# Narrow causal attention on one Trainium2 core: probabilities turned undivided, value products multiplied by inverted sums that a DMA spreads over the partitions

## The reference, cut to what matters

```
x = x + 0.5 * _L0_ffn(layernorm(x))      # narrow causal attention, then 16 experts, top 4
x = x + _L0_attn(layernorm(x))           # heads of 8
x = x + 0.5 * _L0_ffn(layernorm(x))      # the same narrow attention and experts again
x = x + 0.5 * _L1_ffn(layernorm(x))
x = x + _L1_attn(layernorm(x))           # wide attention: heads of 128, two blocks of keys
x = x + 0.5 * _L1_ffn(layernorm(x))
```

```
q, k = rope((h @ wq), (h @ wk)); v = h @ wv      # 32 query heads, 8 key heads of 64
scores = q k^T / 8, causal over 512 positions
attn = softmax(scores)
x = x + (attn @ v) @ wo
```

## Time and profile before

| | us |
|---|---|
| median of 3 runs | 3932.72 (3931.78 to 3938.23) |
| the profiled execution | 3977.27 |
| its span, first to last instruction | 3975.5 |

### The profile page before, as it was taken

One profiled execution on the slowest core, in us unless ns is written; L12 is line 12 of the kernel. 1 busy time (PEld: TensorE's weight loads), 2 busy tenths in 40 slices (PEclk: granted clock), 3 DMA queues, 4 the chain that ended last, 5 costly groups with the idle time before them and its releaser, 6 DMA issues. The chain is left out here.

```text
span 3975.5 us, 62571 instructions
## 1 busy us (share of the span) xinstructions
PE 3386.8 (85%) x21000; PEld 2236.6 (56%) x21002; DVE 2620.2 (66%) x8701; ACT 1915.0 (48%) x5261; POOL 993.6 (25%) x960
## 2 busy tenths in 40 slices
PE   6899999887798698997889999988599567999976
PEld 4566666655454333343666666655355346788864
DVE  6777878665343677774777777766444367777765
ACT  4566666554222166665466666655322113555541
POOL 3212112232344100111221212123244342222213
PEclk9899999888899589998889999988799768999986
DMA  3320400011754422111150310001275600000010
GB/s 120 107 99 22 139 1 1 18 45 42 200 89 81 101 54 54 45 24 40 47 198 7 115 46 1 1 33 42 97 161 91 140 14 1 14 14 4 1 32 22
DMA packets 203909, 234.62 MB, mean 59 GB/s; under 512 B 20358, under 2 KB 190280, under 8 KB 202824
## 3 DMA queue, kind: packets, MB, share of 16 engines
q1 hardware_dynamic: 172648, 190.48, 15.8%
q0 software_dynamic: 30944, 40.14, 6.0%
HBM read 96.03 MB, written 133.73 MB: 58 GB/s over the span
## 5 line engine op out<-in xcount | busy, mean ns | idle before, releaser
L1896 DVE CUSTOM_DVE_ANT_0 bank<-bank,p_mask 128x256 f32<-128x256 f32 (+3 forms) x1280 | 583.4, 489 | 248.1 <-PE bank L1469 221.1
L1726 ACT ACTIVATE p_prob<-bank,p_small 128x256 f32<-128x256 f32 (+3 forms) x1280 | 649.4, 520 | 174.3 <-DVE p_small L1896 167.4
L1731 ACT ACTIVATE p_prT<-bank 128x512 f32<-128x512 f32 x752 | 429.1, 605 | 460.1 <-PE bank L1478 442.1
L2241 POOL TENSOR_TENSOR p_tm<-p_rope_a,p_rope_b 128x512 f32<-128x512 f32 x192 | 246.2, 1282 | 1407.6 <-DVE p_rope_b L1875 1360.4
L1469 PE MATMUL bank<-p_k,p_q 64*128 64x256 f32 (+3 forms) x3840 | 534.4, 353 | 17.9 <-ACT p_prob L1726 16.7
L1478 PE MATMUL bank<-g_ident,p_prob 128*128 128x128 f32 x3008 | 454.7, 292 | 78.5 <-ACT p_v L1712 36.7
L1478 PEld LDWEIGHTS bank<-g_ident,p_prob 128*128 128x128 f32 x3008 | 344.6, 146 | 173.9 <-issue 46.8
L1487 PE MATMUL bank<-p_prT,p_v 128*64 128x512 f32 (+1 forms) x1504 | 425.9, 609 | 0.3 <-ACT p_prT L1731 0.3
L1905 DVE TENSOR_SCALAR p_prob<-p_prob,p_small 128x256 f32<-128x256 f32 (+3 forms) x1280 | 416.5, 389 | 11.3
L1469 PEld LDWEIGHTS bank<-p_k,p_q 64*128 64x128 f32 (+1 forms) x3840 | 344.3, 192 | 117.1 <-issue 66.4
L1942 DVE TENSOR_REDUCE p_nmax<-bank 128x1 f32<-128x512 f32 x512 | 325.1, 685 | 95.2 <-PE bank L1528 89.5
(11 more groups left out here) (289 smaller groups left out, 6243.5 us busy)
## 6 DMA issues: line engine op xcount, KB each, us to landing
sorted<-p_blank SPq DMA_DIRECT2D x32, 2304.0 KB, 18.9
p_w<-in_L_ffn_w SPq DMA_DIRECT2D x96, 256.0 KB, 4.4
p_h_in<-sorted SPq DMA_DIRECT2D x158, 144.0 KB
p_k_st<-k_saved SPq DMA_DIRECT2D x16, 288.0 KB
p_q_st<-q_saved SPq DMA_DIRECT2D x16, 288.0 KB
g_stage<-in_L_ffn_wq SPq DMA_DIRECT2D x8, 512.0 KB, 4.4
g_stage<-in_L_ffn_wo SPq DMA_DIRECT2D x16, 256.0 KB, 5.2
second_sum<-g_res SPq DMA_DIRECT2D x8, 512.0 KB, 6.1
```

The costliest lines, as they stand in the source:

```text
L1726: act.activation(s.prob.ap[:, 0:s.o.w], s.use.ap[:, 0:s.o.w], ACT.Exp, bias=sm[:, 0, j:j + 1], scale=-1.0, accum_out=sm[:, 1, j:j + 1]).th ...
L1731: act.activation(s.prT.ap, s.use.ap, ACT.Copy).then_inc(s.use.free[0].sem)
L1896: dve.tensor_tensor_reduce(x, x, A.mask[:, A.mask.shape[1] - o.w:], -1.0, FAR, ALU.add, ALU.min, o.sm.ap[:, 0, h.j:h.j + 1]).then_inc(made)
```

## The change

In the narrow phases the probabilities are no longer multiplied by the inverted sums. They are turned as they are. The list of a narrow step becomes: scores of heads 0 and 1, `weigh` (PE only), `invert` of `prev` (one DVE reciprocal of four sums into a buffer that both groups of a t share), exponentials, `divide` (DVE: weighed bank times `oT`, into `oT`, frees the bank), a piece, `project_out`, `spread` (when `prev` has g = 1), a piece, scores 2 and 3, two turns, `parts` (ACT: `oT` to `oT_hi`; POOL: the rest to `oT_lo`), exponentials, a piece, further turns, exponentials, a piece.

`spread` brings the 8 inverted sums per query to the layout of the weighed bank: PE turns 128 x 8 to 8 x 128 through a `tring` bank, DVE copies it to SBUF, SP writes it to DRAM, waits for that, and reads each group's 4 x 128 row back into 64 partitions of `oT` at once, two DMAs. `oT`, `oT_hi` and `oT_lo` are single buffers; `project_out` waits for the low part by POOL.

In all three attention phases the copy of v by ACT comes one step of the list before the rotation of k and no longer behind it; the rotation waits for the copy, and DVE frees that bank.

```diff
@@ attention
+        def invert(o):
+            s = self.step("invert", A)
+            if o.g == 0:
+                o.inverse = inverse.take()
+            else:
+                o.inverse = pend[-1].inverse
...
+        def spread(o):
+            s = self.step("spread", A)
+            s.inverse, s.inverted, s.use, s.rows, s.x = o.inverse, o.inverted, wring.take(), inverse_rows.take(), oT.take()
...
+        def divide(wd):
+            s = self.step("divide", A)
+            s.use, s.x, s.filled = wd.use, wd.spread.x, wd.spread.filled
@@ the step
                 if prev:
-                    normalise(prev)
-                beside()
+                    (normalise if wide else invert)(prev)
+                if wide:
+                    beside()
                 exponentials()
                 if weighed:
-                    weighed = low_parts(weighed)
+                    (low_parts if wide else divide)(weighed)
...
+                else:
+                    beside()
                 if settled:
                     project_out(settled)
                     settled = None
+                if prev and prev.g == nk - 1 and not wide:
+                    spread(prev)
                 beside()
...
                 for kt in range(0, min(2, nturn)):
                     turn(prev, kt)
+                if weighed and not wide:
+                    low_parts(weighed)
                 exponentials()
@@ tensor_program
+        elif s.kind == "spread":
+            w.wait_ge(s.use.before, s.inverted)
+            pe.transpose(s.use.ap[0:A.nk * KV, 0:P], s.inverse.ap.rearrange("p g j -> p (g j)"), ident[:, :]).then_inc(s.use.full[0].sem)
@@ scalar_program
         elif s.kind == "v_copy":
-            w.wait_ge(s.rotated, s.v.after)
+            w.wait_ge(s.kb.full, s.v.after)
...
+        elif s.kind == "parts":
+            w.wait_ge(s.divided, s.hi.after)
+            act.activation(s.hi.ap, s.x.ap, ACT.Copy).then_inc(made)
@@ vector_program
+        elif s.kind == "invert":
+            dve.reciprocal(s.inverse.ap[:, o.g, :], o.sm.ap[:, 1, :]).then_inc(made)
+        elif s.kind == "spread":
+            w.wait_ge(s.use.full, s.rows.after)
+            dve.tensor_copy(s.rows.ap, s.use.ap[0:A.nk * KV, 0:P]).then_inc(s.use.free[0].sem)
+        elif s.kind == "divide":
+            w.wait_ge(s.use.full, s.filled)
+            dve.tensor_tensor(s.x.ap, s.use.ap, s.x.ap, ALU.mult).then_inc(s.use.free[0].sem)
@@ pool_program
+        elif s.kind == "parts":
+            w.wait_ge(s.hi_made, s.lo.after)
+            pool.tensor_tensor(s.lo.ap, s.x.ap, s.hi.ap.bitcast(F32), ALU.subtract).then_inc(made)
@@ sync_program
+        elif s.kind == "spread":
+            w.wait_ge(s.use.free, s.place_read)
+            sp.dma_start(s.place, s.rows.ap).then_inc(s.saved[0].sem, 16)
+            w.wait_ge(s.saved, s.x.after)
+            for g in range(A.nk):
+                row = s.place[g * KV:(g + 1) * KV, :].rearrange("j q -> (j q)").unsqueeze(0)
+                sp.dma_start(s.x.ap[cols(g * A.hd, A.hd), :], row.to_broadcast([A.hd, KV * P])).then_inc(s.filled[0].sem, 16)
```

More of the change, by code:

```diff
@@ L350, in attention @@
         prT = Ring([sb(f"prT{i}", [P, KV * P])[:, :] for i in range(8)])
-        oT_hi, oT_lo = (Ring([sb(f"oT_{s}{i}", [P, KV * P], F32R)[:, :] for i in range(2)]) for s in ("hi", "lo"))
+        oT_hi, oT_lo = (Ring([sb(f"oT_{s}{i}", [P, KV * P], F32R)[:, :] for i in range(2 if wide else 1)]) for s in ("hi", "lo"))
+        if not wide:
+            oT = Ring([sb("oT", [P, KV * P])[:, :]])
+            inverse = Ring([sb(f"inverse{i}", [P, nk, KV])[:, :, :] for i in range(3)])
+            inverse_rows = Ring([sb(f"inverse_rows{i}", [nk * KV, P])[:, :] for i in range(2)])
+            rows_saved, oT_filled = self.count(f"p{ph}_rows_saved"), self.count(f"p{ph}_oT_filled")
+            saved_read = [None, None]
         small = Ring([sb(f"small{i}", [P, 3, KV])[:, :, :] for i in range(3)])
@@ L414, in products_of @@
             w_used[c] = kb.full
+            v = self.step("v_copy", A)
+            v.t, v.kb, v.v, v.made = t, kb, unit.v, self.scalar_made.up()
+            unit.v_made.append(v.made)
             yield
             k = self.step("k_rotate", A)
-            k.t, k.kb, k.qb, k.ra, k.rb, k.tm = t, kb, qb, s.ra, s.rb, s.tm
-            k.rotated = self.vector_made.up()
+            k.t, k.kb, k.qb, k.ra, k.rb, k.tm, k.v_made = t, kb, qb, s.ra, s.rb, s.tm, v.made
             k.q_sum, k.k_sum = self.pool_made.up(), self.pool_made.up()
@@ L422, in products_of @@
             rotated[t] = s.tm, k.k_sum
[L423 to L427, removed]
             yield
-            if not wide:
-                yield
+            yield
         def turned_of(unit, t, rotated):
@@ L499, in weigh @@
             s = self.step("weigh", A)
-            s.os, s.use, s.hi, s.lo = os, wring.take(), oT_hi.take(), oT_lo.take()
-            s.hi_made = self.scalar_made.up()
+            s.os, s.use = os, wring.take()
+            if not wide:
+                s.spread = pend_spread[-1]
+            if wide:
+                s.hi, s.lo, s.hi_made = oT_hi.take(), oT_lo.take(), self.scalar_made.up()
             for o in os:
@@ L507, in weigh @@
             return s
+        def divide(wd):
+            s = self.step("divide", A)
+            s.use, s.x, s.filled = wd.use, wd.spread.x, wd.spread.filled
         def low_parts(wd):
-            s = self.step("low_parts", A)
-            s.use, s.hi, s.lo, s.hi_made = wd.use, wd.hi, wd.lo, wd.hi_made
+            if wide:
+                s = self.step("low_parts", A)
+                s.use, s.hi, s.lo, s.hi_made = wd.use, wd.hi, wd.lo, wd.hi_made
+                wd.made = wd.use.free
+            else:
+                s = self.step("parts", A)
+                s.x, s.divided = wd.spread.x, wd.use.free
+                s.hi, s.lo = wd.hi, wd.lo = oT_hi.take(), oT_lo.take()
+                s.hi_made, s.lo_made = self.scalar_made.up(), self.pool_made.up()
+                s.x.users.append(s.lo_made)
+                wd.made = s.lo_made
             return wd
@@ L517, in project_out @@
             s.o, s.hi, s.lo, s.use = o, wd.hi, wd.lo, wring.take()
-            s.ready = [wd.use.free, o_ready[o.c]]
+            s.ready = [wd.made, o_ready[o.c]]
             wd.hi.users.append(s.use.full)
@@ L621, in attention @@
             project_out(settled)
[L622 to L627, removed]
+        for os in ([full] if full else []) + [pend + [prev]]:
+            if os[-1] is prev:
+                (normalise if wide else invert)(prev)
+                if not wide:
+                    spread(prev)
+                for kt in range(prev.nkt):
+                    turn(prev, kt)
+            weighed = weigh(os)
+            if not wide:
+                divide(weighed)
+            project_out(low_parts(weighed))
         self.routing = itertools.chain(*routing)
```

30 lines of the change are left out of this document (25 added, 5 removed).

## The result

| | median us | lowest to highest |
|---|---|---|
| before, same chip | 3935.47 | 3931.78 to 3952.59 |
| changed | 4061.72 | 4053.59 to 4071.79 |

The ratio is 1.0313, 95% interval 1.0274 to 1.0353: slower, by some 123 us (between the means of the four runs; the two medians of the table lie 126 apart). Forecast were +102 us and 4035, in a range of 3945 to 4120. The profiled execution of the changed kernel took 4071.79 us (span 4070.0).

The account below looks back on a forecast made before the run. PE was taken to bound steady units. Steady units 65.7, early 12, routing 12, tails 4 and clock 10 gave +103.7 us on the profiled execution, scaled to +102.5: forecast 4035 us, range 3945 to 4120.

Parts of the forecast that it names:

- PE bounds a steady unit, DVE's products there cost nothing: Steady unit: PE busy 49.3 of 52.2 us; removing DVE's products, about 13 us of DVE per unit, counted at nothing.
- The low part behind the turns: Before `project_out`: PE waits for the chain through ACT's `parts` and POOL's subtraction, 2.95 us per unit, bounds 2.2 and 3.6.
- the last section of the prediction: Expected signs: PE waits of 1.75, 0.95 and 0.25 us before `project_out`, none on v's copy, unit 55 to 56 us.
- `spread` on PE: Four transposes of 128 x 8 per unit on PE, 0.2 us each: 0.8 us, bounds 0.6 and 1.5.
- One more bank: Ring of four: first turn behind `spread` needs the q turn's bank back from DVE; 0.5 us per unit, bounds 0 and 1.4.
- The round trip: Inverted sums through DRAM, 6.2 to 6.5 us in all, make `divide` late at t = 0; PE waits 0.5 us per unit.
- I count no delay: Clears of `sorted` follow `spread` of t = 2, next `spread` over 12 us behind them: no delay to its DMAs.
- The copy of v: ACT's copy no longer waits for the rotation: PE's longest wait on it goes, -1.1 us per unit, bounds 0 and 2.3.
- Sum of a steady unit: 2.95 + 0.8 + 0.5 + 0.5 - 1.1 = +3.65 us per steady unit; eighteen of them 65.7.
- Routing quarters: Eight units with routing: gain from DVE's products gone, against `divide` and its DMA; +1.5 us each, 12 in all.
- Clock: New PE waits of 1.75 us, about 26, lower the granted clock one time in four, 1.6 us each: 10 us.
- Forecast: Total +103.7 us on the profiled execution, scaled to +102.5 on the runs: 4035 us, chance 0.52.

Follow-up runs that it names:

- third group: Kernel before with the early copy of v, undivided with `parts` ahead of the turns only in the last quarter of the heads: 0.9844 to before, 3902.23 us.
- the later group: Changed kernel unaltered, on the same chip as its variants: 1.0373 to before; kernel before with only the copy of v moved earlier: 0.9853.

## Why the prediction was right, and where not

- *PE bounds a steady unit, DVE's products there cost nothing*: right to 0.4 us of 49.7, by the kernel without products.
- *The low part behind the turns*: 1.75, 0.95 and 0.25, sum 2.95. These are delays against the starts of before, and from the start of the last turns before it to `project_out` PE now takes 1.76, 0.83 and 0.15 us longer (3.31 against 1.55, 3.74 against 2.91, 3.75 against 3.60), sum 2.74. The mechanism, the three places and the sizes were right, and moving `parts` took the waits away. What the last section of the prediction got wrong is that it named the same three numbers as the lengths of PE's waits. Those are 1.53, 1.34 and 0.74, sum 3.61: two of the starts of before held idle time on the copy of v, 0.51 and 0.80, and part of it is now idle time on the low part.
- *`spread` on PE*: 0.8, measured 0.76 as busy time (50.03 less 49.27), whose ends are modelled. From start to start the transpose behind the first `project_out` pushed the k turns back by 0.11 us only.
- *One more bank*: 0.5, measured 0.82 of waits (0.50 and 0.32 for the low part of q).
- *The round trip*: 5.5 us for its DMAs, measured 4.6; 0.5 per unit from it, measured none in an undisturbed unit; in a routing quarter it was late by more (third group), which the forecast had not counted apart. The Trainium skill ("DMA: Bandwidth & Descriptors", section "Anatomy of one DMA — SWDGE (gpsimd) path") gave 4.6 as an estimate, and in sum the trace agrees, though with 1.3 for the write and 3.3 for the reads.
- *"I count no delay" for the clears*: this step failed. I placed them by the list, and forgot that the loads of weights come at the same place of it, and that the next write of `spread` has to wait behind all of them; in the kernel before no such write stood behind them. Four units were 2.5 to 4.5 us longer. Clears apart or no DMAs gave 10 to 12 us back.
- *The copy of v*: -1.1 on top of what was inside the low part's terms. All three waits went. In place of the one of 1.12 stands now one of 0.66 for the rotation, so in the changed kernel's sum it is about -0.5 and not -1.1; made alone, in the kernel before, it is -2.5 per unit, and no wait for the rotation takes its place.
- *Sum of a steady unit*: +3.65, measured +3.5 undisturbed and +4.6 on average over the 18. The sum came out closer than its terms: the smaller gain from the copy of v was made up by the round trip, which cost nothing there.
- *Routing quarters*: +12 us, measured -16.6 in the first pair of profiles, where one quarter stood at a clock of 0.91 against 0.86. In the later group the changed kernel's were 292 and 288, against 267 and 273 with the copy of v. The relief of DVE is worth 27 to 37 us per quarter by itself, and the rest of the change takes most or all of it back. I had the two sides, but each far too small; their difference is not resolved by these profiles, since quarters of one kernel differ by 20 us.
- *Clock*: units of 56.7 beside 55.7 also come without the round trip, and the two units shown above tie them to a granted clock of 0.97, about 1 us each. In the changed kernel eight of the 18 steady units stand at 0.95 to 0.97, with 51.4 to 52.5 us of PE busy against 50.0, and none in the kernel before. One fall in four was too few, but a fall alone cost about 1 us and not my 1.6.
- *Forecast*: 102 us of 123, and 103.7 against 94.5 in the pair of profiles. That it came so near is in part luck: the steady units cost 17 us more than their own terms (10 of which I had put down to the clock) and the experts' stretch 15, which is not the change's, while the routing quarters came out 29 us under. The steady units alone carry 83, and the change lost more against what was within reach than against before.

## What to carry to other kernels

Look for what the moved work newly stands behind: two short operations, one each on ACT and POOL, made PE wait 3.6 us a unit only because they were listed behind copies that wait for PE, and moving one step of the list took all of it away in an undisturbed unit. Split a change into parts before judging it; here one part gains 1.5% and the rest loses 5% (1.0373 over 0.9853 on one chip). A wait for a DMA in an engine's own list also stops that engine from running ahead, so see what else it used to issue early.

## What the runs showed of the hardware

A write of 4 KB behind two DMAs of 2304 KB and 1280 KB of weights on the same queue took 2.58 us to issue and let its readers go 9.9 us after its start, against 0.30 and 1.3 us in an undisturbed unit. The same unit of work kept PE busy 51.5 us at a granted clock of 0.97 and 50.0 at 1.00. POOL's subtraction of 128 x 512 took 1.27 us, at hand-overs of 0.1 to 0.2 us, and was still the better choice: the same operation given to DVE, which had 24 us to spare per unit, cost 3.4 us per unit, because DVE's other results, for which PE waits, then stood behind it in its list.
